# Router logits of a conv, attention and mixture-of-experts kernel: the tokens as stationary operand

## The chip, the cores and the metric

One core of one Trainium2 chip runs the whole program. The metric is the device time of one launch in microseconds (us). The core has five engines with instruction streams of their own: TensorE (PE; its weight loads are listed as PEld), VectorE (DVE), ScalarE (ACT), GpSimd (POOL) and SyncE (SP), which here only issues DMAs.

## The reference

The input `x` is 4 images of 128 channels by 1024 positions, all in float32. Three blocks follow each other.

```
x = x + Wp( softmax(q k^T / sqrt(128)) v )           # q, k, v from group_norm(x); 1024x1024 scores per image
t = tokens(x)                                        # 4 x 1024 tokens of 128 channels
t = t + linear_attention(layer_norm(t)) @ W_out + b_out   # 4 heads, softmax of the keys over the tokens
n = layer_norm(t)
logits = n @ router_w.T                              # 8 experts
rw, re = top_k(softmax(logits), 2); rw = rw / rw.sum()
ffn = n + sum_e combine[:, e] * (gelu(n @ w1[e] + b1[e]) @ w2[e] + b2[e])
out = t + ffn
```

The change concerns one line of it: `logits = n @ router_w.T`, for 4 x 1024 tokens and 8 experts.

## The kernel before

Most products are done in three parts: each float32 operand is split into a high and a low part of type fp32r, and `product3` (lines 1400 to 1405) adds high by high, high by low and low by high in one PSUM bank (128x512 float32).

The work is software-pipelined over the images. `batch(place, b, la, lc)` does three things interleaved: the convolutional attention of image b, the linear attention of image la = b-1, and the second norm, the routing and the residual of image lc = b-2. The first image has an `opening_batch`, the second a `batch` without routing, and images 2 and 3 run in a hardware loop, `with pe.Fori(2, B)` on PE and in the same way on the other engines. I call these two passes the second-image pass and the third-image pass (counting from zero). After them come the experts: for each image 16 steps (8 experts, two halves of the tokens), 64 in all, into which `TAIL_AT` puts the routing of image 2 (and the linear attention of image 3) by step number and `END_AT` the routing of image 3. The order of the work on every engine is written out by hand in these functions; nothing reorders it.

PSUM has eight banks. Everything that is not scores goes through named units in banks: `ring` 0 to 3 in the passes, and in the expert stage also two banks of `scores`. The table `LOOP_UNITS` says which bank each unit of a looped pass takes, in PE's order; in the expert stage `place_of` deals the banks out in turn, `TAIL_FIRST` being the first. `open_unit` lets PE wait until the previous unit of the same bank is drained, that is, read out by ACT or DVE. So a unit's bank decides whose reader PE waits for. In a pass the units `T0a` to `T7b` are the transposed probabilities of eight row blocks (ACT writes the high part, `turn_probs`, then DVE the low part, line 1026), `PV0/PV1` and `OT0/OT1` the attention output and its transpose (`OT` is drained by DVE's `residual`, line 1045), `g` the key-token product (drained by `take_g`), `u` and `w` the transposed first and second norm, `z` the transposed residual, `kT` the keys, `p` their softmax turned back, `c` the transposed expert shares.

The router's part of a pass runs so. When `w0` and `w1` are drained (the transposed norm, `wT_hi` and `wT_lo`, 128 channels by 1024 tokens), PE's `logits` makes two units `lg0` and `lg1`: the router, padded with zeros to 128x128 (`rt_hi`, `rt_lo`), is stationary and 512 tokens stream, three matmuls a unit. Eight of the 128 output rows are logits. ACT's `take_logits` copies 8x512 of each into `lgT`. After the scores of row block 5 and the two `u` units, PE's `turn_logits` turns them back with eight transposes of 8x128 into the unit `lT` (128 tokens by 8 tiles by 8 experts). DVE's `less_top` (lines 1143, 1144) then takes each token's maximum and subtracts it, which drains `lT`, and a chain of some twenty small DVE operations (`part_a`, `part_b`, `part_c`) finds the two best experts and their shares. In DVE's order `less_top` stands after the low parts of `T3` and before the row maximum of row block 5 (line 1019); `part_a` follows, then the key maximum, `part_b`, `part_c`, and the low parts of `T4` and `T5`. POOL's `add_bout` (line 583) waits until `z1` is filled.

Of the kernel before, what the change touches and what calls it, by code (L numbers as in the profile page):

```python
# [23 lines left out]
FP32 = mybir.dt.float32  # L24
# [8 lines left out]
E = 8  # L33
# [15 lines left out]
ROUTING = dict(o=["o0", "o1"], w=["w0", "w1"], lg=["lg0", "lg1"], z=["z0", "z1"], c=["c0", "c1"])  # L49
# [15 lines left out]
TAIL_UNITS = (ATTENTION["T"][6] + ["ctx"] + ATTENTION["T"][7] + ["m2", "m3", "PV1"] + ROUTING["o"]  # L65
              + ["OT1"] + ROUTING["w"] + LINEAR["u"] + ROUTING["lg"] + ["lT"] + LINEAR["kT"]
              + ROUTING["z"] + LINEAR["p"] + ROUTING["c"] + ["g"])

END_UNITS = (["ctx", "m2", "m3"] + ROUTING["o"] + ROUTING["w"] + ROUTING["lg"] + ["lT"]
# [20 lines left out]
LINEAR_CHAIN, ROUTING_CHAIN = 5, 17  # L90
# [42 lines left out]
def conv_attention_moe(nc, x, gn_scale, gn_bias, wq, bq, wk, bk, wv, bv, wp, bp,  # L133
# [27 lines left out]
    with ctx:  # L161
# [3 lines left out]
        def sem(name):  # L165
# [12 lines left out]
        wq_hi, wq_lo, wk_hi, wk_lo, rt_hi, rt_lo = (  # L178
            sb(n, [C, C], FP32R) for n in ("wq_hi", "wq_lo", "wk_hi", "wk_lo",
                                           "rt_hi", "rt_lo"))  # L180
# [47 lines left out]
        rr = sb("rr", [P, 6, TILES])  # L228
        comb = sb("comb", [P, 2, P])
# [8 lines left out]
        lgT = p1[0:E, :]  # L238
# [409 lines left out]
        def _(act):  # L648
# [66 lines left out]
            def take_logits(place):  # L715
                for n in range(HALVES):
                    unit = f"lg{n}"
                    wait_filled(act, place, unit)
                    act.activation(half(lgT, n), ps(place, unit)[0:E, :], ACT.Copy
                                   ).then_inc(drained[place.bank(unit)], 1)  # L720

# [41 lines left out]
            def batch(place, after_place, b, la, lc):  # L763
# [20 lines left out]
                if lc is not None:  # L784
                    take_logits(place)
# [46 lines left out]
            def experts(m, between):  # L832
# [14 lines left out]
                (TAIL_AT["lg"], lambda: take_logits(TAIL)),  # L847
# [5 lines left out]
                (END_AT["lg"], lambda: take_logits(END)),  # L853
# [9 lines left out]
        def _(dve):  # L863
# [99 lines left out]
            dve.memset(rt_hi[:, :].bitcast(FP32), 0.0)  # L963
            dve.memset(rt_lo[:, :].bitcast(FP32), 0.0)
# [17 lines left out]
            def setup_rest():  # L982
# [5 lines left out]
                after(dve.tensor_copy(rt_hi[:, 0:E], ps(FIRST, "rowsT")[:, 0:E]))  # L988
                dve.tensor_tensor(rt_lo[:, 0:E], ps(FIRST, "rowsT")[:, 0:E], rt_hi[:, 0:E].bitcast(FP32),
# [142 lines left out]
            def route(place, lc):  # L1132
# [255 lines left out]
        def _(pe):  # L1388
# [176 lines left out]
            def logits(place, lb):  # L1565
                for n in range(HALVES):
                    wait_drained(pe, place, f"w{n}")
                    whole(place, f"lg{n}", (rt_hi[:, :], rt_lo[:, :]), w_of(lb, n))

            def turn_logits(place):  # L1570
                wait_drained(pe, place, "lg0")
                wait_drained(pe, place, "lg1")
                dst = open_unit(place, "lT")
                apart(pe)
                for j in range(TILES):
                    last = pe.transpose(dst[:, j * E:(j + 1) * E], tile(lgT, j), ident[0:E, 0:E])
                fill(place, "lT", last)
# [56 lines left out]
            def batch(place, b, la, lc):  # L1634
# [41 lines left out]
                if lc is not None:  # L1676
                    turn_logits(place)
                    turn_z(place, lc)
# [17 lines left out]
            with pe.Fori(2, B) as b:  # L1696
                batch(loop_place(b), b, b - 1, b - 2)
# [100 lines left out]
```

## Time and profile before

| | |
|---|---|
| median of 3 runs | 334.31 us (334.0 to 335.09) |
| profiled execution, its own time | 334.79 us |
| its span | 332.9 us |
| busy: PE, DVE, ACT, POOL | 91%, 77%, 58%, 31% |
| chain that ended last: PE, DVE, issue, ACT | 59%, 23%, 7%, 4% |

The page of the profile divides the span among the engines, then follows the chain of work that ended last back to the start. A timeline row has the start and the length in us, the engine, the line, the operation, and in brackets how long the engine was idle before it and what ended that. PE's span can be read in five stretches: the first two images to 91.8 us, the second-image pass to 147.6, the third-image pass to 202.5, the expert stage with the TAIL work to about 265 and with the END work to about 293.5, and the rest of the experts.

### The profile page before, as it was taken

Reading aid. Unit: us, or ns where it says so; the run is one execution under the profiler, and the core shown is the slowest. Engines: PE = TensorE matmul, PEld = TensorE weight load, DVE = VectorE, ACT = ScalarE, POOL = GpSimd, SP = SyncE. Lnnn points to the kernel's source line nnn. Section 1 sums busy time; section 2 is a strip of 40 time slices with the busy share of each in tenths; the row PEclk is TensorE's granted clock in tenths of the full one; section 3 lists DMA queues with packets and bytes.
Section 4 is the critical chain, followed back from the end, with each engine's and each line's share of the span. In section 5 each row is a group of like instructions: output and inputs, shape, how many; then the busy total and the mean of one; then the engine's idle time right before and its main releaser. Section 6 shows DMA issues by size and latency. Waiting matters only on the chain.

```text
span 332.9 us, 5172 instructions
## 1 busy us (share of the span) xinstructions
PE 301.8 (91%) x1569; PEld 235.6 (71%) x1569; DVE 256.0 (77%) x623; ACT 191.8 (58%) x332; POOL 102.1 (31%) x154
## 2 busy tenths in 40 slices
PE   2887989989989899789989996999999997999995
PEld 2776868777968677577768785867757774666884
DVE  4799686678686798987687885787688685777995
ACT  3356474676570586445277656458567435856883
POOL 2345350059102664500636200089120037000000
PEclk9999999999999999999999999999999999999999
DMA  5902000010000011000000106396520692239511
GB/s 152 300 0 66 0 1 2 0 66 0 0 3 0 0 65 64 2 12 0 0 1 0 63 12 201 132 376 255 172 91 0 177 372 112 71 116 385 189 33 63
DMA packets 12757, 29.58 MB, mean 89 GB/s; under 512 B 2192, under 2 KB 5952, under 8 KB 10816
## 3 DMA queue, kind: packets, MB, share of 16 engines
q1 hardware_dynamic: 12448, 29.00, 25.3%
q10 hardware_dynamic: 288, 0.33, 0.3%
q8 instruction: 10, 0.16, 0.2%
q14 instruction: 11, 0.09, 0.1%
HBM read 24.73 MB, written 4.59 MB: 88 GB/s over the span
## 4 chain that ended last, share of the span: by engine, by line
PE 59%; DVE 23%; issue 7%; ACT 4%; DMA 3%; POOL 2%; SPq 1%; DVEq 0%; POOLq 0%; ACTq 0%
PE ring L1403 7%; PE ring L1721 6%; PE ring L1405 6%; PE ring L1404 6%; PE ring L1418 6%; PE scores L1403 6%; PE scores L1405 6%; PE scores L1404 6%; DVE prob L1019 4%; DVE pT_lo L1026 4%; PE ring L1555 2%; DVE lst L1056 2%; ACT prob L674 2%; PE ring L1533 2%; DVE t L1045 1%
## 5 line engine op out<-in xcount | busy, mean ns | idle before, releaser
L819 ACT ACTIVATE gel<-scores,b_c 128x512 f32<-128x512 f32 x64 | 43.9, 688 | 35.6 <-PE scores L1405 32.5
L1019 DVE TENSOR_SCALAR_CACHE_REDUCE prob<-scores 128x1024 f32<-128x1024 f32 x32 | 38.9, 1215 | 12.1 <-PE scores L1405 12.0
L1026 DVE TENSOR_TENSOR pT_lo<-ring,pT_hi 128x512 fp32r<-128x512 f32 x64 | 40.7, 681 | 8.1 <-ACT pT_hi L680 7.6
L556 POOL TENSOR_SCALAR rstd<-lmv 128x8 f32<-128x8 f32 x8 | 2.1, 260 | 135.3 <-DVE lmv L1062 135.3
L680 ACT ACTIVATE pT_hi<-ring 128x512 fp32r<-128x512 f32 x64 | 34.3, 598 | 14.5 <-PE ring L1418 14.5
L674 ACT ACTIVATE prob<-prob,row_max 128x1024 f32<-128x1024 f32 x32 | 36.8, 1151 | 9.5 <-DVE prob L1019 9.3
L1418 PE MATMUL ring<-ident,prob 128*128 128x128 f32 x256 | 33.9, 276 | 8.2 <-ACT prob L674 5.8
L1418 PEld LDWEIGHTS ring<-ident,prob 128*128 128x128 f32 x256 | 28.4, 140 | 14.0 <-ACT prob L674 6.1
L1403 PE MATMUL scores<-wT_hi,w_hi 128*128 128x512 f32 x64 | 34.2, 534 | 0.0
L1403 PE MATMUL scores<-k_both,q_hi 128*128 128x512 f32 x64 | 27.3, 427 | 0.9 <-DVE k_both L1004 0.9
L1403 PE MATMUL ring<-pT_hi,v_hi 128*128 128x512 f32 x64 | 26.7, 417 | 1.2 <-DVE pT_lo L1026 1.2
L1404 PE MATMUL scores<-wT_lo,w_hi 128*128 128x512 f32 x64 | 25.1, 393 | 0.0
L1405 PE MATMUL scores<-k_both,q_lo 128*128 128x512 f32 x64 | 25.1, 393 | 0.0
L1405 PE MATMUL scores<-wT_hi,w_lo 128*128 128x512 f32 x64 | 25.1, 392 | 0.0
L1404 PE MATMUL scores<-k_both,q_hi 128*128 128x512 f32 x64 | 25.1, 392 | 0.0
L1405 PE MATMUL ring<-pT_hi,v_lo 128*128 128x512 f32 x64 | 25.0, 390 | 0.0
L1404 PE MATMUL ring<-pT_lo,v_hi 128*128 128x512 f32 x64 | 25.0, 390 | 0.0
L684 ACT ACTIVATE o_s<-ring 128x512 f32<-128x512 f32 x8 | 4.8, 598 | 30.4 <-PE ring L1405 30.4
L564 POOL TENSOR_SCALAR u<-t,rstd 128x128 f32<-128x128 f32 x32 | 16.4, 531 | 0.9 <-POOL rstd L560 0.9
L1403 PEld LDWEIGHTS scores<-wT_hi,w_hi 128*128 128x128 f32 x64 | 12.1, 189 | 6.1 <-issue 4.3
L1404 PEld LDWEIGHTS scores<-wT_lo,w_hi 128*128 128x128 f32 x64 | 12.1, 189 | 5.4 <-issue 4.3
L1403 PEld LDWEIGHTS ring<-pT_hi,v_hi 128*128 128x128 f32 x64 | 12.0, 188 | 4.9 <-issue 1.2
(297 smaller groups left out, 725.9 us busy)
## 6 DMA issues: line engine op xcount, KB each, us to landing
pT_hi<-scratch_s SPq DMA_DIRECT2D x8, 1024.0 KB, 6.6
prob<-scratch_s SPq DMA_DIRECT2D x4, 1024.0 KB, 7.7
k_both<-scratch_s SPq DMA_DIRECT2D x3, 1024.0 KB, 6.7
z_in<-scratch_z SPq DMA_DIRECT2D x8, 256.0 KB, 3.2
out_dram<-out_s SPq DMA_DIRECT2D x8, 256.0 KB, 2.2
xb<-in_x_dram SPq DMA_DIRECT2D x3, 512.0 KB, 3.1
scratch_z<-out_s SPq DMA_DIRECT2D x2, 512.0 KB, 2.8
k_both<-scratch_s SPq DMA_DIRECT2D x4, 256.0 KB, 4.4
```

What stands on the lines that cost most here:

```text
L564: last = pool.tensor_scalar(dst[:, j, :], src[:, j, :], neg[:, j:j + 1], std[:, j:j + 1], ALU.add, ALU.mult)
L674: act.activation(prob[:, i % 2, :], prob[:, i % 2, :], ACT.Exp, bias=row_max[:, i:i + 1], scale=-1.0, accum_out=row_sum[:, 0, i:i + 1]).th ...
L680: act.activation(tile_group(pT_hi, n, i), as_tiles(ps(place, unit)), ACT.Copy).then_inc(p_hi_made, 1)
L819: act.activation(half(gel, s % 2), scores[:, s % 2, :], ACT.Gelu, bias=b1_c[:, s % E:s % E + 1]).then_inc(e_gelu, 1)
L1019: dve.tensor_scalar(prob[:, i % 2, :], scores[:, 2 * (i % 2):2 * (i % 2) + 2, :].rearrange("p a t -> p (a t)"), -1.0, None, ALU.mult, ALU. ...
L1026: dve.tensor_tensor(tile_group(pT_lo, n, i), as_tiles(ps(place, unit)), tile_group(pT_hi, n, i).bitcast(FP32), ALU.subtract).then_inc(drai ...
L1056: last = dve.bn_stats(lst[:, j, :], src[:, j, :])
L1403: pe.matmul(dst, lh, rh, start=start, stop=False)
L1404: pe.matmul(dst, lh, rl, start=False, stop=False)
L1405: return pe.matmul(dst, ll, rh, start=False, stop=stop)
L1418: last = pe.transpose(dst[0:t.shape[-1], j * step:j * step + rows], t, ident[0:rows, 0:rows])
L1721: last = pe.matmul(dst, tile(w2_s, e), hs_ring[step % RING], start=False, stop=e == E - 1)
```

## The change

`logits` is turned round. For each of the eight tiles of 128 tokens, the tokens are stationary and the router streams as 16 columns: first `wT_hi` against `[high, low]`, then `wT_lo` against `[high, 0]`, both into the same 16 columns of `lT`. The tokens come out on the partitions, so `lg0`, `lg1`, `take_logits` and `turn_logits` are gone. The high-part and low-part columns are added by a new DVE reduction into `logit` (64 values a partition), and `less_top` now reads that from SBUF. `lT` is filled at the place of `logits` and its bank is used again by `u1`. The table `LOOP_UNITS` is dealt anew behind `T2b`, `TAIL_FIRST` is 0 in place of 2, and PE's hardware loop over images 2 and 3 is written out.

```diff
-                  lg0=0, lg1=1, T3a=2, T3b=3, u0=0, u1=1, lT=2, z0=3, z1=0, kT0=1, kT1=2, PV0=3, T4a=0,
-                  T4b=1, T5a=2, T5b=3, p0=0, p1=1, c0=2, c1=3, g=0, OT0=1)
-TAIL_FIRST = 2
+                  lT=0, T3a=1, T3b=2, u0=3, u1=0, z0=1, z1=2, kT0=3, kT1=0, PV0=1, T4a=2, T4b=3, T5a=0,
+                  T5b=1, p0=2, p1=3, c0=0, c1=1, g=2, OT0=3)
+TAIL_FIRST = 0
...
-LINEAR_CHAIN, ROUTING_CHAIN = 5, 17
+LINEAR_CHAIN, ROUTING_CHAIN = 5, 18
...
+        router4 = sb("router4", [C, 4, E], FP32R)
+        logit = sb("logit", [P, TILES, E])
...
-            dve.memset(rt_hi[:, :].bitcast(FP32), 0.0)
-            dve.memset(rt_lo[:, :].bitcast(FP32), 0.0)
+            dve.memset(router4[:, 3, :].bitcast(FP32), 0.0)
...
-                after(dve.tensor_copy(rt_hi[:, 0:E], ps(FIRST, "rowsT")[:, 0:E]))
-                dve.tensor_tensor(rt_lo[:, 0:E], ps(FIRST, "rowsT")[:, 0:E], rt_hi[:, 0:E].bitcast(FP32),
+                router_hi, router_lo = router4[:, 0, :], router4[:, 1, :]
+                dve.tensor_copy(router4[:, 2, :], ps(FIRST, "rowsT")[:, 0:E])
+                after(dve.tensor_copy(router_hi, ps(FIRST, "rowsT")[:, 0:E]))
+                dve.tensor_tensor(router_lo, ps(FIRST, "rowsT")[:, 0:E], router_hi.bitcast(FP32),
...
-                    logits = ps(place, "lT")[:, 0:TILES * E].rearrange("p (j e) -> p j e", e=E)
-                    link("routing", lc, red(top, logits, AX.X, ALU.max, negate=True))
-                    tt(less, logits, over(top), ALU.add).then_inc(drained[place.bank("lT")], 1)
+                    parts = ps(place, "lT")[:, 0:2 * TILES * E].rearrange("p (j k e) -> p j e k", k=2, e=E)
+                    link("routing", lc, red(logit[:, :, :], parts, AX.X, ALU.add))
+                    link("routing", lc, red(top, logit[:, :, :], AX.X, ALU.max, negate=True))
+                    tt(less, logit[:, :, :], over(top), ALU.add).then_inc(drained[place.bank("lT")], 1)
...
             def logits(place, lb):
+                dst = open_unit(place, "lT")
+                both, high = (router4[:, 2 * n:2 * n + 2, :].rearrange("p k e -> p (k e)") for n in range(2))
                 for n in range(HALVES):
                     wait_drained(pe, place, f"w{n}")
-                    whole(place, f"lg{n}", (rt_hi[:, :], rt_lo[:, :]), w_of(lb, n))
-
-            def turn_logits(place):
-                wait_drained(pe, place, "lg0")
-                wait_drained(pe, place, "lg1")
-                dst = open_unit(place, "lT")
-                apart(pe)
-                for j in range(TILES):
-                    last = pe.transpose(dst[:, j * E:(j + 1) * E], tile(lgT, j), ident[0:E, 0:E])
+                    for j in range(QUAD):
+                        i = n * QUAD + j
+                        cols = dst[:, i * 2 * E:(i + 1) * 2 * E]
+                        pe.matmul(cols, wT_hi[:, bass.ds(lb * T + i * P, P)], both, start=True, stop=False)
+                        last = pe.matmul(cols, wT_lo[:, bass.ds(lb * T + i * P, P)], high, start=False, stop=True)
                 fill(place, "lT", last)
...
-            with pe.Fori(2, B) as b:
+            for b in range(2, B):
                 batch(loop_place(b), b, b - 1, b - 2)
```

## Rows read from the trace of the kernel before

**Rows 1.** The chain that ended last: shares of the span by engine
```profile
PE 59%; DVE 23%; issue 7%; ACT 4%; DMA 3%; POOL 2%; SPq 1%; DVEq 0%; POOLq 0%; ACTq 0%
```
**Rows 2.** Waits of PE between 90 and 202 us: total in us, times, longest
```profile
PE ring L1418 <- ACT p L705: 1.3, 1, 1.3
```
**Rows 3.** Timeline of the second-image pass around the logits
```profile
122.52 0.40 PE L1403 MATMUL ring<-wT_hi,rt_hi 128*128 x1
...
123.90 1.04 PE L1418 MATMUL ring<-ident,prob 128*128 128x128 f32 x8
...
125.20 1.29 DVE L1026 TENSOR_TENSOR pT_lo<-ring,pT_hi 128x512 fp32r<-128x512 f32 x2
...
127.12 0.66 PE L1576 MATMUL ring<-ident,p 8*128 8x8 f32 x8
127.71 0.86 PEld L1418 LDWEIGHTS ring<-ident,t 128*128 128x128 f32 x8
...
127.81 0.22 DVE L1143 TENSOR_REDUCE rr<-ring 128x8 f32<-128x64 f32 x1 [1.33 <-PE ring L1576]
128.07 0.22 DVE L1144 TENSOR_TENSOR rt<-ring,rr 128x64 f32<-128x64 f32 x1
128.28 1.23 DVE L1019 TENSOR_SCALAR_CACHE_REDUCE prob<-scores 128x1024 f32<-128x1024 f32 x1
...
128.89 2.38 POOL L583 TENSOR_TENSOR t<-t,bout_row 128x1024 f32<-128x1024 f32 x1 [4.37 <-PE ring L1418]
...
129.52 1.80 DVE L1149 TENSOR_SCALAR rt<-rt 128x64 f32<-128x64 f32 x1
```
**Rows 4.** Weight loads around a product with one column
```profile
17.96 0.30 PEld L1412 LDWEIGHTS ring<-cols,ctx_s 128*128 128x128 f32 x2
18.18 0.19 PEld L1403 LDWEIGHTS scores<-k_both,q_hi 128*128 128x128 f32 x1
```
**Rows 5.** Second-image pass, DVE's routing and what follows it
```profile
136.82 1.13 POOL L548 TENSOR_SCALAR xb<-xb,cols 128x1024 f32<-128x1024 f32 x1
...
137.01 1.00 DVE L1157 TENSOR_TENSOR rt<-rt,rr 128x64 f32<-128x64 f32 x1
...
141.31 2.48 DVE L1026 TENSOR_TENSOR pT_lo<-ring,pT_hi 128x512 fp32r<-128x512 f32 x4
```
**Rows 6.** Timeline from the second-image pass into the third-image pass
```profile
147.60 1.04 PE L1418 MATMUL ring<-ident,prob 128*128 128x128 f32 x8
148.14 1.13 DVE L1045 SCALAR_TENSOR_TENSOR t<-ring,row_sum,xT 128x128 f32<-128x128 f32 x4 [0.48 <-PE ring L1418]
148.24 1.08 ACT L680 ACTIVATE pT_hi<-ring 128x512 fp32r<-128x512 f32 x2 [2.03 <-PE ring L1418]
...
149.21 1.15 ACT L674 ACTIVATE prob<-prob,row_max 128x1024 f32<-128x1024 f32 x1
149.32 0.51 PE L1403 MATMUL ring<-h_hi,wq_hi 128*128 128x512 f32 x1 [0.46 <-DVE t L1045]
...
150.58 1.09 PE L1418 MATMUL ring<-ident,prob 128*128 128x128 f32 x8 [0.29 <-ACT prob L674]
```
**Rows 7.** Third-image pass: low parts of T4 and T5
```profile
193.34 2.48 DVE L1026 TENSOR_TENSOR pT_lo<-ring,pT_hi 128x512 fp32r<-128x512 f32 x4
```
**Rows 8.** The chain between the third-image pass and the experts
```profile
202.78 3.97 DMA k_both<-scratch_s
```
**Rows 9.** The last steps of the routing of image 3, PE and DVE
```profile
282.70 0.51 PE L1403 MATMUL ring<-wT_hi,rt_hi 128*128 128x512 f32 x1 [0.59 <-DVE wT_lo L995]
...
287.63 0.22 DVE L1143 TENSOR_REDUCE rr<-scores 128x8 f32<-128x64 f32 x1
...
293.45 0.33 PE L1418 MATMUL ring<-ident,comb 128*128 128x128 f32 x1 [0.42 <-DVE comb L1179]
```
**Rows 10.** A DVE operation with two SBUF operands beside POOL's, TAIL
```profile
242.12 2.19 DVE L1152 TENSOR_TENSOR rt<-rt,rr 128x64 f32<-128x64 f32 x1
```
**Rows 11.** DVE's split of the router in the first image's batch
```profile
27.61 0.16 DVE L988 CAST rt_hi<-ring 128x8 fp32r<-128x8 f32 x1
```

More of the change, by code:

```diff
@@ L48 @@
 LINEAR = dict(u=["u0", "u1"], kT=["kT0", "kT1"], p=["p0", "p1"])
-ROUTING = dict(o=["o0", "o1"], w=["w0", "w1"], lg=["lg0", "lg1"], z=["z0", "z1"], c=["c0", "c1"])
+ROUTING = dict(o=["o0", "o1"], w=["w0", "w1"], z=["z0", "z1"], c=["c0", "c1"])
 FIRST_UNITS = dict(q0=3, k0=0, k1=1, q1=2, wvT=3, wpv=0, bias_o=1, v0=2, v1=3, T0a=0, T0b=1, l1qT=2,
@@ L59 @@
                   OT1=1, v0=0, v1=1, T0a=2, T0b=3, T1a=0, T1b=1, xT0=2, xT1=3, w0=0, w1=1, T2a=2, T2b=3,
[L60 to L64 removed]
+                  lT=0, T3a=1, T3b=2, u0=3, u1=0, z0=1, z1=2, kT0=3, kT1=0, PV0=1, T4a=2, T4b=3, T5a=0,
+                  T5b=1, p0=2, p1=3, c0=0, c1=1, g=2, OT0=3)
+TAIL_FIRST = 0
 TAIL_UNITS = (ATTENTION["T"][6] + ["ctx"] + ATTENTION["T"][7] + ["m2", "m3", "PV1"] + ROUTING["o"]
[L66 removed]
+              + ["OT1"] + ROUTING["w"] + LINEAR["u"] + ["lT"] + LINEAR["kT"]
               + ROUTING["z"] + LINEAR["p"] + ROUTING["c"] + ["g"])
[L69 removed]
+END_UNITS = (["ctx", "m2", "m3"] + ROUTING["o"] + ROUTING["w"] + ["lT"]
              + ROUTING["z"] + ROUTING["c"])
@@ L177, in conv_attention_moe @@
         wpv = sb("wpv", [C, C])
-        wq_hi, wq_lo, wk_hi, wk_lo, rt_hi, rt_lo = (
-            sb(n, [C, C], FP32R) for n in ("wq_hi", "wq_lo", "wk_hi", "wk_lo",
-                                           "rt_hi", "rt_lo"))
+        wq_hi, wq_lo, wk_hi, wk_lo = (sb(n, [C, C], FP32R) for n in ("wq_hi", "wq_lo", "wk_hi", "wk_lo"))
+        router4 = sb("router4", [C, 4, E], FP32R)
         bout_row = sb("bout_row", [P, C])
@@ L713, in turn_keys @@
                                    ).then_inc(drained[place.bank(unit)], 1)
[L715 to L720, printed above, removed]
             def route_exp(place, lb):
@@ L783, in batch @@
                 turn_probs(place, 2)
-                if lc is not None:
-                    take_logits(place)
                 turn_probs(place, 3)
@@ L846, in _ @@
                 *((TAIL_AT["u" + str(n)], lambda n=n: turn_u(TAIL, n)) for n in range(2)),
-                (TAIL_AT["lg"], lambda: take_logits(TAIL)),
                 (TAIL_AT["exp"], lambda: route_exp(TAIL, lc)),
@@ L852, in _ @@
                 *((END_AT["w" + str(n)], lambda n=n: turn_normed(END, "w", n, w_halves(la), w_hi_made)) for n in range(2)),
-                (END_AT["lg"], lambda: take_logits(END)),
                 (END_AT["exp"], lambda: route_exp(END, la)),
@@ L1676, in batch @@
                 if lc is not None:
-                    turn_logits(place)
                     turn_z(place, lc)
@@ L1753, in _ @@
                 (TAIL_AT["lg"], lambda: logits(TAIL, lc)),
-                (TAIL_AT["lT"], lambda: turn_logits(TAIL)),
                 (TAIL_AT["kT"], lambda: keys(TAIL)),
@@ L1765, in _ @@
                 (END_AT["lg"], lambda: logits(END, la)),
-                (END_AT["lT"], lambda: turn_logits(END)),
                 (END_AT["z"], lambda: turn_z(END, la)),
```

1 line of the change is left out of this document (removed).

## The prediction

> **What bounds the kernel now.** I read the page's engine shares first, then the chain that ended last, then PE's waits, then the timeline around each place that the diff touches. PE is busy nine tenths of the span and carries 59% of the chain, DVE 23% [rows 1]. In the expert stage the chain is nearly all PE. In the two looped passes it changes sides: PE streams, but at the logits the chain leaves PE and stays on DVE for 15 us. The reader sees it in the timeline: PE's eight small transposes end at 127.71, DVE, which had idled 1.33 us for them, takes the maximum at once, subtracts, and only then does the row maximum of block 5 [rows 3]. DVE then works through routing, key maximum and shares until the low parts of T4 and T5 [rows 5], on which the share transposes and the next scores wait. PE meanwhile has slack of its own: one wait of 1.3 us for the key softmax [rows 2]. From the third-image pass into the experts the chain runs over DVE's share copy, stores and a broadcast load of 3.97 us [rows 8], not over PE.
>
> **PE's own work.** Removed for each image: six matmuls of 512 columns, 122.52 to 123.90, 1.38 us, and eight transposes, 127.12 to 127.71, 0.59 us [rows 3]. Added: sixteen pairs of a 128x128 load and a 16-column matmul. The nearest row is a product with one column: its two loads span 0.30 at 0.19 each, so they start 0.11 apart, and the next load follows after another 0.11 [rows 4]. A pair thus costs a load, 0.112, however short the matmul: 16 x 0.112 = 1.79 us. Lower bound: the pace of the small transposes, 0.59 / 8 = 0.074, gives 1.18. Upper bound: loads not overlapped at all, 0.19 each [rows 4], gives 3.04. I take 1.79, its row having the same 128x128 operand. So PE's gain is 0.18 us an image, with 0.41 more at the logits and 0.59 less later.
>
> The Trainium skill, "TensorE: Matmul & The Clock Gate", section "Back-to-back issue gap", lists matmuls of 1 to 64 columns at about 60 cycles, 25 ns; by that the sixteen would be an estimated 0.4 us. Its section on LDWEIGHTS gives columns / 1.2 in ns, 107 for 128, and says that the row count doesn't matter; [rows 4] agree with 107, the eight-row transposes of [rows 3] came faster than it allows. The first would make the change a gain; it is the first rival below, which has its price from rows.
>
> **DVE's own work.** One reduction more. Line 1143 reads 64 values a partition in 0.22 and the next starts 0.26 later [rows 3]; the new one reads 128. Line 1026 does 512 in about 0.62 (1.29 for two, [rows 3]), 1.2 ns each, so 64 more are 0.07: 0.33 a step (between 0.26 and 0.52). `less_top` becomes 0.33 + 0.26 + 0.22 = 0.81 us. Its last operation now has both operands in SBUF. Such an operation took 2.19 us beside a POOL operation [rows 10] instead of 0.22; here POOL has been idle 4.37 us before line 583 [rows 3], so I cost the wait at nothing; if POOL moved there it would be up to 2.2. The skill's page "SBUF — State Buffer", section "Who interferes with whom", states the same as a rule: a DVE instruction with two SBUF inputs contends with a GpSimd instruction that reads SBUF.
>
> **The two looped passes.** The sixteen pairs make T3's transposes 0.41 late, and ACT's high and DVE's low parts with them: the low parts end at about 126.90 instead of 126.49 (125.20 + 1.29). `less_top` needs nothing more from PE, so `lT` is drained at 126.95 + 0.81 = 127.75. Two things follow. DVE's row maximum starts at about 127.8 instead of 128.28, 0.5 early. But `u1` now sits in `lT`'s bank: PE would be ready for it at 127.0 and waits until 127.8; with its four transposes of 0.109 `z` starts at 128.24 instead of 127.71, 0.5 late. POOL's `add_bout` starts on `z1`, hence also 0.5 late, 129.4, and ends at 131.75.
> DVE then gets the first operation of `part_a` in before POOL (it had stood 1.80 us behind POOL, [rows 3]) but a later one with two SBUF operands stands until POOL's end, itself 0.5 later. In the second-image pass every further POOL operation is 0.5 late too, and each holds one DVE operation, as line 1157 was held till the end of line 548, 137.95 [rows 5]. Going through them one by one, four more short operations fit in under cover before POOL's end at 138.4; the low parts of T4 start at 141.1 instead of 141.31: -0.2. In the third-image pass DVE is bound by ACT's high part of T4, which hangs on PE's 0.5: 193.25 instead of 193.34 [rows 7]: -0.1. Bounds for each: -0.5 (DVE keeps all of it) and +0.5 (PE's lateness decides). PE's 0.5 at the end of the third pass lies behind the stores and the load of [rows 8].
>
> **The bank table between the two passes.** The new table ends a pass with `g` in bank 2 and `OT0` in bank 3, and begins the next with `T6a` in 2 and `T6b` in 3. Before, `OT0`'s bank went to `q0`, and one sees PE stand there 0.46 us until line 1045 is done, at 149.27 [rows 6]. Now `T6b` stands there. Its four transposes start at 149.33 instead of 148.04 (147.60 and four times 0.11); ACT's second copy of T6 starts at 149.95, the exponential of block 7 at 150.47 instead of 149.21, and T7's transposes, which wait for it at 150.58 [rows 6], at 151.83. `q0`, whose bank is free now, moves up but its ACT copy stands behind the exponential, so `k0` is late as well. That is +1.25 us, with 15 us of unbroken PE work behind it. Bounds: 0 and 1.4. It happens once: the pass before the loop ends on the old banks, and `TAIL_FIRST` 0 gives T6 the banks of `c0` and `c1`, long drained.
>
> **Experts.** TAIL: PE loses 0.59 and gains 0.41, on the chain: -0.2. END: the second half of the logits starts when `w1` is drained, 282.70 [rows 9]; eight pairs are about 0.15 longer than three matmuls, and with them the GELU and DVE's start on the routing at 287.63. From there DVE works unbroken to the shares, PE waiting 0.42 for them [rows 9]; the new reduction adds 0.33. The 0.59 of the removed transposes only lengthens that wait. END: +0.45.
> **The rest.** One more 128x8 copy on DVE's busy stretch in the first image, 0.16 long and partly overlapped [rows 11]: +0.1. ACT's two copies an image lie in ACT's idle time: nothing; were ACT late there, 1.2 us back. The written-out PE loop: at its edge T6's transposes at 147.60 have no idle time before them [rows 6], so nothing to gain; bounds -0.3 and +0.3.
>
> **Sum.** 0.1 - 0.2 + 1.25 - 0.1 - 0.2 + 0.45 = +1.3 us. The profiled execution took 334.79 (span 332.9), so 336.1 in its terms; the median of before is 334.31, so I predict 335.6.
>
> **Rivals.**
> Short loads: the pair runs at the small transposes' 0.074. Then TAIL gains 0.6 more, END 0.3, the passes 0.2 each: 335.6 - 1.3 = 334.3. For it: load and 16 columns are short. Against: [rows 4]. Chance 0.14.
> The bank wait is covered: T7's delay is taken up before DVE's next work: 335.6 - 1.25 = 334.35. Against: PE runs unbroken after 150.58. Chance 0.15.
> The other side, faster: POOL's block. In both passes line 1149 stood about 1.6 us behind `add_bout` (1.80 for an operation of 0.2). If DVE, 0.5 earlier, gets all five operations of `part_a` (1.3 us) in before POOL's start, each pass gains 1.6 instead of 0.15: 335.6 - 2.9 = 332.7. It decides if POOL starts after 130.3; I have 129.4. Chance 0.12.
> Slow loads: 0.19 a pair. TAIL +1.25, END +0.6, the passes about 0.8 each: 339.1. Chance 0.09.
> My forecast has 0.50, its own range 334.9 to 336.6.
>
> **How the numbers follow.** A change under 0.3%, 1 us, can't be told from none here; the limits are 333.3 and 335.3. Slower: 0.43 of my case, slow loads and a little of the rest, 0.53. Same: the two 334.3 cases and the lower edge of mine, 0.33. Faster: POOL's case and edges, 0.14. The range leaves out slow loads and most of POOL's case: 333.4 to 337.6.
>
> **What would show it.** In the trace after: sixteen matmuls of 16 columns 0.11 apart; PE idle before `u1`, ended by `rt` (line 1144's successor), 0.7 to 0.8 us, in both passes; PE idle about 0.7 us or more before `T6b` ended by DVE `t`, once, and T7 of that pass waiting for ACT over 1.2 us later than now; DVE's row maximum of block 5 no longer behind `z`; in END PE's wait for `comb` 1.2 us instead of 0.42. I am wrong if the pairs are not load-bound, if the second-to-third pass distance does not grow, or if DVE's `part_a` runs free of POOL.

## The result and the profile after

| | before | after |
|---|---|---|
| median of 4 runs each | 334.15 us (333.57 to 335.09) | 338.27 us (337.24 to 338.94) |
| profiled execution, span | 334.79, 332.9 us | 338.56, 336.5 us |
| granted clock of PE, mean of the span | 1.0 | 0.99 |

The changed kernel is slower: the ratio is 1.0115 with a 95% interval of 1.0091 to 1.0139, some 3.8 us (the medians lie 4.1 apart). I had forecast 335.6 and a range up to 337.6. The sign is right, the size is not.

The page of after: busy shares, the chain (its shares stand against [rows 1]), and the granted clock in tenths over 40 slices.

```profile
PE 303.2 (90%) x1577; PEld 238.1 (71%) x1577; DVE 257.2 (76%) x627; ACT 187.7 (56%) x324; POOL 101.9 (30%) x154
PE 64%; DVE 21%; issue 6%; ACT 5%; POOL 2%; DMA 1%; DVEq 0%; ACTq 0%; POOLq 0%
PEclk9999999999999999989999999999999999899999
```

The last of these lines holds what I had not looked for: two of the 40 slices are an 8 instead of a 9. The text comes back to them below. First the steps that I had foreseen. The pairs of load and matmul of the second-image pass, PE's timeline (to be read against [rows 3] and [rows 4]):

```profile
122.34 0.26 PE L1565 MATMUL ring<-router,wT_lo 128*128 128x16 f32 x1
122.45 0.26 PE L1564 MATMUL ring<-router,wT_hi 128*128 128x16 f32 x1
122.56 0.26 PE L1565 MATMUL ring<-router,wT_lo 128*128 128x16 f32 x1
...
123.90 0.26 PE L1565 MATMUL ring<-router,wT_lo 128*128 128x16 f32 x1
```

Load and matmul together go at one every 0.11 us. The first of the sixteen starts at 122.31 and the work behind them at 124.01: 1.70 us. In the same pass, the engines around `u1` (PE first, then DVE, then POOL):

```profile
127.48 0.63 PE L1408 MATMUL ring<-ident,u 128*128 128x128 f32 x4 [0.55 <-DVE rt L1134]
...
126.54 0.28 DVE L1132 TENSOR_REDUCE logit<-ring 128x64 f32<-128x128 f32 x1
...
128.92 0.16 DVE L1139 TENSOR_SCALAR rt<-rt 128x64 f32<-128x64 f32 x1
129.12 2.41 DVE L1140 TENSOR_TENSOR rt<-rt,falling 128x64 f32<-128x64 f32 x1
...
129.07 2.38 POOL L582 TENSOR_TENSOR t<-t,bout_row 128x1024 f32<-128x1024 f32 x1 [4.84 <-PE ring L1408]
```

`u1` waits 0.55 us for `less_top`. DVE gets one operation of `part_a` in ahead of POOL (128.92), and the next stands until POOL's end (129.12 to 131.53). All this is as foreseen. Three lines of PE's timeline at the pass boundary, against [rows 6]:

```profile
148.76 0.63 PE L1408 MATMUL ring<-ident,prob 128*128 128x128 f32 x4
...
150.22 0.66 PE L1408 MATMUL ring<-ident,prob 128*128 128x128 f32 x4 [0.83 <-DVE t L1034]
...
152.69 0.55 PE L1408 MATMUL ring<-ident,prob 128*128 128x128 f32 x3 [0.89 <-ACT prob L673]
```

`T6b` now stands behind `OT0`'s reader, and T7 waits for the exponential. From the start of `OT0`'s transposes to the start of `q1` it is 155.79 - 148.12 = 7.67 us in after and 153.69 - 147.17 = 6.52 us in before: +1.15.

Then the two 8s, which are two falls of the granted clock. The stretch with the key softmax's transposes in the second-image pass, as windows (start and end, length, busy time and count of PE, PEld, DVE, ACT, POOL, then the granted clock), with the wait ahead of it:

```profile
142.00:144.00 2.00, 1.92 (x11) 1.56 (x11) 2.00 (x4) 0.79 (x2) 0.00 (x0) 0.64 0.00 0
144.00:146.00 2.00, 2.00 (x6) 1.61 (x6) 1.26 (x4) 1.50 (x3) 0.00 (x0) 0.50 0.03 8
146.00:148.00 2.00, 2.00 (x17) 1.92 (x17) 1.23 (x2) 0.15 (x2) 0.00 (x0) 1.00 0.19 49
```
```profile
142.08 1.68 PE L1408 MATMUL ring<-ident,p 128*128 128x128 f32 x8 [2.18 <-DVE pT_lo L1015]
...
144.49 0.63 PE L1394 MATMUL scores<-k_both,q_hi 128*128 128x512 f32 x1
144.91 0.63 PE L1395 MATMUL scores<-k_both,q_lo 128*128 128x512 f32 x1
```

The same windows of before have the clock at 1.00. In after PE is granted 0.50 of full speed, that is the lower of its two levels (1.2 instead of 2.4 GHz): matmuls of 512 columns start 0.42 apart where 0.23 is usual. And in the experts:

```profile
284.00:286.00 2.00, 1.79 (x12) 1.65 (x13) 1.36 (x3) 0.22 (x1) 0.00 (x0) 0.98 0.00 0
286.00:288.00 2.00, 2.00 (x5) 0.89 (x3) 1.16 (x2) 1.21 (x2) 0.00 (x0) 0.50 0.00 0
288.00:290.00 2.00, 2.00 (x7) 1.41 (x5) 0.74 (x2) 0.47 (x1) 0.00 (x0) 0.66 0.15 56
```
```profile
278.89 0.66 PE L1408 MATMUL scores<-ident,w_n 128*128 128x128 f32 x4 [1.85 <-POOL w_n L563]
...
284.21 0.28 PE L1564 MATMUL ring<-router,wT_hi 128*128 128x16 f32 x1 [0.49 <-DVE wT_lo L984]
```

The two profiles can be compared stretch by stretch, as distances between the starts of the same PE work (after less before):

| stretch | after less before, us |
|---|---|
| first images, up to `q0` of the second-image pass (93.31 and 93.64) | -0.3 |
| second-image pass, up to `OT0` | +1.3, of which the fall +1.0 |
| boundary, `OT0` to `q1` | +1.15 |
| third-image pass, up to its `OT0` | +0.3 |
| TAIL, up to END's m3 product | -0.9 |
| END, up to `comb`'s transposes | +2.05, of which the fall 1.65 |

They add up to the 3.6 us between the spans. The first row is no effect that can be told: profiles of kernels with the code of before differ by up to 1.1 us there. What a fall costs is read from later profiles with the same waits and full clock: 53.8 us for the pass where after has 54.8, and 27.9 for END where after has 29.5. Without the two falls the rest behind `q0` is +1.2, near my +1.3. The falls are the other 2.7.

### The profile page after: what moved, and what is told of

The parts are those of the page before. It is cut to its first block, busy times and chain, and to the rows that moved or that the text cites. A ratio compares the mean times of both kernels' runs of the same rounds, so it can differ in the third digit from the quotient of the medians.

```text
span 336.5 us, 5099 instructions
## 1 busy us (share of the span) xinstructions
PE 303.2 (90%) x1577; PEld 238.1 (71%) x1577; DVE 257.2 (76%) x627; ACT 187.7 (56%) x324; POOL 101.9 (30%) x154
## 4 chain that ended last, share of the span: by engine, by line
PE 64%; DVE 21%; issue 6%; ACT 5%; POOL 2%; DMA 1%; DVEq 0%; ACTq 0%; POOLq 0%
PE ring L1408 7%; PE ring L1393 7%; PE ring L1709 7%; PE ring L1395 6%; PE ring L1394 6%; PE scores L1393 6%; PE scores L1395 6%; PE scores L1394 6%; DVE prob L1008 3%; DVE pT_lo L1015 3%; PE ring L1545 2%; PE ring L1523 2%; DVE lst L1045 2%; ACT prob L673 2%; PE ring L1510 2%
## 5 line engine op out<-in xcount | busy, mean ns | idle before, releaser
L1393 PE MATMUL scores<-wT_hi,w_hi 128*128 128x512 f32 x64 | 35.6, 556 | 0.7 <-ACT gel L809 0.7
L1393 PE MATMUL scores<-k_both,q_hi 128*128 128x512 f32 x64 | 27.8, 435 | 0.9 <-DVE k_both L993 0.9
L1394 PE MATMUL scores<-k_both,q_hi 128*128 128x512 f32 x64 | 25.3, 396 | 0.0
```

What stands on the lines that cost most here:

```text
L1393: pe.matmul(dst, lh, rh, start=start, stop=False)
L1394: pe.matmul(dst, lh, rl, start=False, stop=False)
```

## The experiments

An execution has a mean granted clock of 0.998 or more, of 0.993 to 0.995, or of 0.990. The profiled ones of these groups show no fall, one fall and two falls. So I count executions at 0.996 or less as "with a fall"; where it lies, only the profiled ones tell. The kernel before, run again beside every experiment, has 13 of 104; their median is 335.4 us against 334.0 for the rest, so a fall costs about 1.4 us in it. I call the kernel of the next run, the change with a bank table that keeps its new waits out, the one with the sound table.

**The bank table undone.** The changed logits stay; the units behind `T2b` get banks that leave `T6b` clear of `OT0` and `u1` clear of `lT`.

```diff
-                  lT=0, T3a=1, T3b=2, u0=3, u1=0, z0=1, z1=2, kT0=3, kT1=0, PV0=1, T4a=2, T4b=3, T5a=0,
-                  T5b=1, p0=2, p1=3, c0=0, c1=1, g=2, OT0=3)
-TAIL_FIRST = 0
+                  lT=0, T3a=2, T3b=3, u0=1, u1=2, z0=3, z1=0, kT0=1, kT1=2, PV0=3, T4a=0, T4b=1, T5a=2,
+                  T5b=3, p0=0, p1=1, c0=2, c1=3, g=0, OT0=1)
+TAIL_FIRST = 2
```

> The changed kernel with a bank table that keeps lT out of u1's way (T3a=2, T3b=3, u0=1, u1=2) and ends a pass as before (g=0, OT0=1), TAIL_FIRST 2. Theory (bank waits plus two falls of the granted clock): PE's wait of 0.55 us before u1 and of 0.83 us before T6b are gone, the distance from the second to the third pass shrinks by 1.1 us; PE is then even earlier at the key transposes, waits there for DVE over 2 us, and the granted clock still falls, in the pass and at the end of the routing of image 3: about 337.1 us. Rival 1 (the bank table is all of it): 334.5. Rival 2 (the written-out loop or the DVE reduction is what costs): 338.2, unchanged.

Measured: 334.56 us, ratio 1.0004 (0.9984 to 1.0023), 4 of 12 executions with a fall. The first rival was right, and my theory that both falls would stay was wrong: the table was the price. All the rest of the change costs between -0.5 and +0.8 us, nothing that can be told. The profile has full clock in the pass, and it shows what the table had changed there. PE's eight transposes of `u` run through, POOL starts at 128.32, and DVE's operation stands behind it as it did before:

```profile
126.32 1.04 PE L1408 MATMUL ring<-ident,u 128*128 128x128 f32 x8
...
128.90 1.84 DVE L1139 TENSOR_SCALAR rt<-rt 128x64 f32<-128x64 f32 x1
...
128.32 2.37 POOL L582 TENSOR_TENSOR t<-t,bout_row 128x1024 f32<-128x1024 f32 x1 [4.10 <-PE ring L1408]
```

In this kernel PE waits twice later on (1.3 for ACT's `p`, then 1.2 for DVE's `pT_lo`), as in before [rows 2]. In after, whose pass starts 0.33 sooner in its profile than in that of before (93.31 and 93.64), DVE got ahead and delivered the key maximum sooner: ACT's `p` starts at 135.85 (before 136.88, so 0.7 sooner in the pass). PE's wait for it vanishes, and PE stands one long wait of 2.18 ahead of `p0` instead, since the low parts it waits for begin at 141.25 (before 141.31, so 0.27 later in the pass). This chain from `u1`'s bank to the long wait is read from the profiles; a table with `u1` alone behind `lT` was not tried. `T6b`'s wait can't be its cause, as it comes 8 us later. The last windows of END still show a fall here (282 to 286), behind a wait of 0.5:

```profile
280.00:282.00 2.00, 1.51 (x14) 1.42 (x13) 2.00 (x4) 0.65 (x2) 0.24 (x1) 1.00 0.00 0
282.00:284.00 2.00, 2.00 (x10) 1.66 (x10) 0.58 (x1) 0.21 (x1) 0.00 (x0) 0.66 0.00 0
284.00:286.00 2.00, 2.00 (x4) 0.97 (x3) 1.49 (x3) 0.99 (x2) 0.00 (x0) 0.50 0.00 0
```

**The loop written out, in the kernel before.**

```diff
-            with pe.Fori(2, B) as b:
+            for b in range(2, B):
```

> The kernel before with PE's loop over images 2 and 3 written out and nothing else. Theory: no effect, 334.2 within 0.5 us, clock 1.0 throughout. Rival (the longer instruction stream is fetched late and PE stands for it): 335.5 to 337, with PE idle times that no semaphore ends in the two passes.

Measured: 334.94, ratio 1.0019 (0.9999 to 1.0039), 4 of 12 with a fall. That is between nothing and 0.4%, a little over what I had expected, and the clock was not full throughout as I had said. The run before holds the written-out loop too and leaves it at most 0.8 us of the 3.8. The opposite half, the changed logits inside the hardware loop, was not tried.

**Only the bank wait, in the kernel before.**

```diff
-                  ... p0=0, p1=1, c0=2, c1=3, g=0, OT0=1)
-TAIL_FIRST = 2
+                  ... p0=0, p1=1, c0=0, c1=1, g=2, OT0=3)
+TAIL_FIRST = 0
```

> The kernel before, its router untouched, with only the last banks of a pass dealt as in the changed kernel (c0=0, c1=1, g=2, OT0=3, TAIL_FIRST 0), so that T6b of the next pass waits for OT0's reader. Theory: PE stands 0.8 us before T6b once, T7 follows 1.1 to 1.3 us late, and nothing takes it back: 335.3 to 335.5. Rival (covered by later slack): 334.2.

Measured: 335.47, ratio 1.0036 (1.0019 to 1.0053), +1.1 us, 2 of 12 with a fall. PE's waits in the two passes now have the new one:

```profile
PE ring L1418 <- DVE t L1045: 0.9, 1, 0.9
```

So the predicted term is real by itself: +1.1 us (0.6 to 1.8) against +1.25, as expected before the run. Falls are no more frequent than in the kernel before.

**PE kept busy ahead of the long wait of the pass.** The changed kernel with the last three-part product of score block 6 done twice more in the second- and third-image passes (it writes the same values).

```diff
+                for _ in range(2 if i == 6 and not (isinstance(b, int) and b < 2) else 0):
+                    last = product3(scores[:, 2 * (i % 2) + 1, :], (tile(q_hi, i), tile(q_lo, i)),
+                                    (half(k_hi, 1), half(k_lo, 1)))
```

> The changed kernel; in the two looped passes PE computes the last three-part product of the scores of row block 6 twice more into the same bank (6 matmuls, 1.4 us), where it stands 2.2 us for DVE's low parts of T4. Theory (the long wait lets the granted clock fall to half, and the next 3.4 us of matmuls run at 0.43 instead of 0.23 us each): clock 1.0 through the second-image pass, the pass about 1 us shorter although it has more work, total 337.2; the fall in the routing of image 3 stays. Rival (the clock falls for another reason, and PE's idle time is just slack): the fall stays, total 338.3 or more.

Measured: 337.21, ratio 1.0086 (1.006 to 1.0113), 1 of 6 with a fall. The wait of 2.2 is down to 0.8, the clock in the pass is 1.00 throughout, and from the pass's first product to `OT0`'s transposes it is 53.8 us, where before has 53.5 and after 54.8. But the added work costs about 1.4 us in the third pass, where nothing had waited so long. It shows the fall of the pass hanging on the wait (1 of 6 executions with a fall, against 10 of 10 of the changed kernel, counted below), and that filling the wait with useless work isn't a cure. One part of my expectation failed: the fall in END should have stayed, and it was gone too, though END was not touched and PE's waits there are the same:

```profile
PE scores L1408 <- POOL w_n L563: 1.8, 1, 1.8
PE ring L1567 <- DVE wT_lo L984: 0.5, 1, 0.5
```
```profile
286.00:288.00 2.00, 2.00 (x9) 1.30 (x8) 0.96 (x2) 1.21 (x2) 0.00 (x0) 1.00 0.00 0
```

So these waits alone don't make END's fall. Why it came in most executions of the changed kernel and in at most one of these six, the runs don't show.

**The router streamed wide.** 64 columns in place of 16, 48 of them zero, at the same 0.11 a pair.

```diff
-        router4 = sb("router4", [C, 4, E], FP32R)
+        router4 = sb("router4", [C, 16, E], FP32R)
...
-                        cols = dst[:, i * 2 * E:(i + 1) * 2 * E]
+                        cols = dst[:, i * 8 * E:(i + 1) * 8 * E]
```

> The changed kernel with the router streamed as 64 columns (48 of them zero) in place of 16, same loads, same pace of 0.11 us a pair since the load covers 64 columns. Theory A (the sixteen pairs leave the array nearly idle, and that with the 0.5 us wait between the halves is what lets the clock fall in the routing of image 3): fewer falls there, 1 to 1.5 us less than the changed kernel. Theory B (the falls come from true idle time of PE before them): nothing changes, 338. If the pairs become longer than 0.11 us, they were not bound by the loads.

Measured: 338.04, ratio 1.0104 (1.0077 to 1.013), 4 of 6 with a fall. Its profiled execution falls in the pass, with the same wait of 2.2:

```profile
142.00:144.00 2.00, 1.85 (x11) 1.23 (x11) 2.00 (x4) 1.20 (x2) 0.00 (x0) 0.82 0.00 0
144.00:146.00 2.00, 2.00 (x6) 1.61 (x6) 1.26 (x4) 1.09 (x2) 0.00 (x0) 0.50 0.03 8
```

The width of the stream doesn't decide in the pass. In END this profile has waits of 2.0 and 0.5 and full clock. With the sound table and 64 columns:

> The changed kernel with the bank table mended and the router streamed as 64 columns (48 of them zero) in place of 16, so that each pair of load and matmul has four times the columns at the same pace of loads. If the fall of the granted clock in END (4 of 12 executions with 16 columns) comes from the short streams, it is gone: 333.4 to 334.3, all executions at 0.998 or more. If it comes from the waits ahead of and behind the logits, a third of the executions keep it and the median stays at 334.3 to 335.0. If the wide matmuls no longer hide behind the loads (pairs over 0.112 apart), it costs 0.5 us or more in five places: 335 or more.

Measured: 333.81, ratio 0.9998 (0.9978 to 1.0018), 3 of 12 with a fall, against 4 of 12 with 16 columns. Nor does it in END, as far as twelve executions can tell.

**PE kept busy ahead of END's w turn.** The changed kernel, the hidden product of step 34 done three times.

```diff
-                product3(scores[:, s % 2, :], (tile(w1_hi, e), tile(w1_lo, e)), w_of(m, h)).then_inc(e_h, 1)
+                for _ in range(3 if m * 2 * E + s == 34 else 1):
+                    last = product3(scores[:, s % 2, :], (tile(w1_hi, e), tile(w1_lo, e)), w_of(m, h))
+                last.then_inc(e_h, 1)
```

> The changed kernel with the expert product of step 34 computed three times into the same bank (6 matmuls more, 1.4 us), where PE stands 1.85 us for POOL's second norm of image 3. Theory B (idle time of PE lets the clock fall): the fall in the routing of image 3 is gone or rare, 1.2 to 1.7 us less than the changed kernel. Theory A (the narrow products do it by themselves): it stays, and the time is that of the changed kernel.

Measured: 336.74, ratio 1.0089 (1.0057 to 1.012), 4 of 6 with a fall; the profiled one has none, though its pass has the wait of 2.2 too:

```profile
PE ring L1408 <- DVE pT_lo L1015: 3.0, 3, 2.2
```
```profile
144.00:146.00 2.00, 2.00 (x14) 1.76 (x13) 1.72 (x5) 1.24 (x2) 0.00 (x0) 1.00 0.03 8
```

Such a wait makes the fall likely, not certain. One of the six has a mean of 0.99, as with two falls, though END's long waits are gone; no profile says where its second one lay. Its two executions without a fall took 334.95 and 335.03, under my 335.6; a part of that is the repeat's own gain, as the next runs show.

**The two together.** Sound table and the repeated product.

> The changed kernel with the bank table mended (T6b no longer behind OT0) and the hidden product of step 34 in END done three times (the repeats write the same values; about 0.6 us of added PE work in all). My theory: the mended table left one loss, a fall of PE's granted clock to half in END in 4 of 12 executions, worth about 1.1 us each; with PE kept busy ahead of END's logits no execution shows it, mean clock 0.998 or more in all, median 333.4 to 334.3, ratio to before 0.998 to 1.000. Rival, the fall comes from the sixteen narrow products themselves: it stays in a third of the executions and the added work is paid on top, 335.0 or more. Rival, the fall only moves to another place: mean clock 0.995 in some executions with no fall at END's logits in the profile, 334.5 to 335.5.

Measured: 333.46, ratio 0.9976 (0.9966 to 0.9986), no fall in 11 executions. It beats even the kernel before, by 0.24%. Was that the changed logits? The same repeat in the kernel before, and this kernel once more beside it:

> The kernel before with the hidden product of step 34 in END done three times, as in the run with the mended table. It tells whether the 0.24% of that run belongs to the added products or to the changed logits with a sound table. My theory: in the kernel before most executions hold full clock through END already, so the repeats have nothing to save; they lie in a wait of PE for w or cost up to 0.6 us: 334.2 to 334.8, ratio 0.999 to 1.002. Rival, the repeats alone make the gain (they shift END's order): 333.5, ratio 0.9976, and the changed logits with a sound table are worth nothing.

> The changed kernel with the mended table and the repeated product of step 34 once more, beside the one above on the same chip. My theory: ratio 0.997 to 0.999 again, all executions at 0.998 or more. If the first result was chance, 0.999 to 1.001.

Measured: 332.96, ratio 0.9954 (0.9932 to 0.9976), 0 of 7 with a fall; and 333.38, ratio 0.9967 (0.9952 to 0.9981), 0 of 11. The rival was right: the repeat makes the gain, and the kernel before gains as much. My reading of the repeat as a cure for the clock alone falls as well. DVE and POOL of the kernel before in END, first without the repeat:

```profile
279.13 2.37 POOL L574 TENSOR_TENSOR t<-t,w_n 128x1024 f32<-128x1024 f32 x1
...
279.49 2.55 DVE L1303 TENSOR_TENSOR hw<-gel,k_both 128x512 f32<-128x512 f32 x1
281.97 0.68 DVE L995 TENSOR_TENSOR wT_lo<-scores,wT_hi 128x512 fp32r<-128x512 f32 x1
```

and with it:

```profile
278.12 2.84 POOL L574 TENSOR_TENSOR t<-t,w_n 128x1024 f32<-128x1024 f32 x1
...
278.02 0.69 DVE L1303 TENSOR_TENSOR hw<-gel,k_both 128x512 f32<-128x512 f32 x1
279.41 0.69 DVE L995 TENSOR_TENSOR wT_lo<-scores,wT_hi 128x512 fp32r<-128x512 f32 x1 [0.70 <-ACT wT_hi L699]
```

The operation to watch is `hw`. Its start stands 0.36 behind POOL's in the one and 0.10 ahead of it in the other, and it takes 2.55 or 0.69 us. What lets it get ahead lies 4 us earlier. Here is the step before, in the kernel before (DVE's previous `hw`, one of POOL's eight `w_n` operations, PE's transposes of the first four):

```profile
275.40 0.73 DVE L1303 TENSOR_TENSOR hw<-gel,k_both 128x512 f32<-128x512 f32 x1 [0.86 <-ACT gel L819]
...
275.59 0.88 POOL L564 TENSOR_SCALAR w_n<-t,rstd 128x128 f32<-128x128 f32 x1
...
277.38 0.66 PE L1418 MATMUL scores<-ident,w_n 128*128 128x128 f32 x4 [1.87 <-POOL w_n L564]
```

and with the repeat:

```profile
275.73 0.69 DVE L1303 TENSOR_TENSOR hw<-gel,k_both 128x512 f32<-128x512 f32 x1 [2.22 <-ACT gel L819]
...
275.83 0.91 POOL L564 TENSOR_SCALAR w_n<-t,rstd 128x128 f32<-128x128 f32 x1
...
275.91 0.66 PE L1418 MATMUL scores<-ident,w_n 128*128 128x128 f32 x4
```

An operation of `w_n` takes 0.45 us, but 0.88 or 0.91 where DVE's `hw` has started just before it. In the kernel before, this is the second operation, so the fourth ends 0.43 late, and with it PE's wait. The six more matmuls fit in the 1.87 that PE waited, and they make the GELU and `hw` later: now `hw` holds up the fifth operation, which the transposes don't need. They start 1.79 behind the start of `w_n` (274.12 to 275.91) instead of 2.23 (275.15 to 277.38), both times 0.05 behind the end of the fourth operation (275.86 and 277.33). With that 0.44 DVE slips in ahead of POOL at the next `hw`. `wT_lo` is there in time, PE's wait of 0.59 [rows 9] is gone, and from END's m3 product to `comb`'s transposes it is 26.5 us instead of 27.5.

**The same wait filled with useful work.** If the order was all, one more real step there should do as well. END's w turns at steps 35 and 35, or 35 and 36, in place of 34 and 35, in the kernel before and in the changed one with the sound table.

```diff
-END_AT = dict(ctx=25, m2=27, m3=28, o=29, st=29, w0=34, w1=35, lg=36, ...
+END_AT = dict(ctx=25, m2=27, m3=28, o=29, st=29, w0=35, w1=35, lg=36, ...
```

> The kernel before with the first w turn of END at step 35 instead of 34 (both turns at step 35), nothing repeated. PE then has one more hidden product and its w2 product (about 1.5 us) to do in the 1.87 us wait for POOL's w_n. My theory: what the repeated product gave came from the order of DVE and POOL: the wait shrinks to 0.4 or less, hw takes 0.69 instead of 2.55, the wait of 0.59 for wT_lo goes; from m3's product to the shares' transposes 26.5 instead of 27.5 and the useful work is not paid twice: 332.0 to 333.3. Rival, full clock needed the added work: the waits go but the time stays within 0.3% of 334.3. Rival, both turns at one step make DVE late: its wT_lo of the second half falls behind POOL again, 334 or more.

> The changed kernel with the mended table and the same move of the first w turn to step 35. My theory: as for the kernel before, 0.4 us above it: 332.4 to 333.7, no execution under clock 0.998. If the clock needs the added work: falls in a third of the executions and 334.3 or more.

> The kernel before with END's w turns at steps 35 and 36 (from 34 and 35). The second turn, a step later, shares its step with the logits, whose second half then waits for DVE's low part right behind its turn: my theory 0.5 to 1.0 us of that wait comes back, 332.8 to 334.0, a little slower than with both turns at 35. Rival: the step between the turns keeps DVE ahead of POOL and it is the faster of the two, by 0.5 or more.

> The changed kernel with the mended table and END's w turns at steps 35 and 36. My theory: as the kernel before with the same steps, within 0.5 us, 333.0 to 334.3; with a wait of 0.5 or more ahead of the second eight narrow matmuls the clock falls in some executions (0.995 or less), which would show that it is the wait beside the narrow matmuls and not the missing repeat that decides.

Measured: 334.82 (1.0004 to 1.0034), 8 of 12 with a fall; 335.18 (1.0005 to 1.0042), 9 of 12; 336.81 (1.0059 to 1.0099), 5 of 6; 336.88 (1.0075 to 1.0142), 6 of 6. My expectation failed in all four, and they are the best evidence on the clock. (For the last of them I had named the other outcome too: falls behind a wait of 0.5 or more.) In the first, `hw` is free of the long POOL operation (0.89) and the 0.59 is gone, as I had said. But the second turn, now right behind the first, waits for POOL. PE's wait for `w_n` from 264 us on, and the windows:

```profile
PE scores L1418 <- POOL w_n L564: 2.0, 2, 1.5
```
```profile
278.00:280.00 2.00, 1.59 (x6) 1.50 (x7) 0.27 (x1) 0.52 (x1) 1.92 (x2) 0.63 0.00 0
280.00:282.00 2.00, 2.00 (x5) 1.00 (x3) 1.22 (x2) 1.28 (x3) 0.80 (x1) 0.51 0.00 0
```

There isn't one narrow matmul near: four transposes stand between waits of 0.47 and 1.49, and the clock is halved behind them. Four executions kept the clock and took 333.73 in the median, eight fell and took 334.95: 1.2 us for the fall. But 333.73 is also the time of the kernel before beside them (333.75), so the useful work at this place gained nothing even at full clock: to get `hw` clear of POOL isn't enough by itself, and what the new wait of 1.49 takes back wasn't measured alone. In the third kernel DVE's second `wT_lo` does fall behind POOL and PE waits 2.7 us; the windows behind it show 0.50:

```profile
282.00:284.00 2.00, 0.37 (x1) 0.37 (x2) 1.57 (x2) 0.00 (x0) 0.42 (x1) 0.85 0.00 0
284.00:286.00 2.00, 2.00 (x6) 1.52 (x6) 0.00 (x0) 0.59 (x1) 0.00 (x0) 0.50 0.00 0
```

**END's routing a step earlier.** The sound table with `lT=37, rA=37, exp=37` in place of 38.

> e1_table with the routing of image 3 one step earlier on DVE and ACT (lT, rA, exp at step 37 instead of 38), which the missing transposes allow. Theory: DVE takes the nine operations in its idle time before the multiply of step 38, PE's wait for the shares (0.4 to 0.5 us) goes, 0.8 to 1.2 us less than e1_table: 333.5, faster than before by 0.7. Rival (DVE becomes late with its multiplies, or the two table loads on ACT now delay the GELUs): 334.6 or more.

Measured: 335.5, ratio 1.0047 (1.0029 to 1.0066), 2 of 6 with a fall; its four others took 335.77 in the median, so this cost has another source than the clock, which I haven't looked for. I had expected 333.5; the rival (334.6 or more) held.

**The changed kernel again**, beside new executions of the kernel before:

> The changed kernel once more, for more executions of it on the chip of the experiments: how many show a granted clock below 1.0 and how long these are against the others. Theory (bank wait and DVE's reduction about +1.3, the rest is the clock): executions at 1.0 lie at 335.5 to 337, those with one fall 1.2 to 1.5 above, those with two as much again; before shows a fall in about a quarter of its executions, this in most. Rival (the clock is not the difference): its executions at clock 1.0 lie at 338 too.

Measured: 338.39, ratio 1.0132 (1.0113 to 1.0152), 6 of 6 with a fall, five of them with two. In its profile both lie at the same places as in the first.

Put in one table, with PE's waits in us as the profiles have them (the longest ones ahead of the places of the two falls):

| kernel | key softmax of the second-image pass | END's w turns and logits | with a fall |
|---|---|---|---|
| before | 1.3 and 1.1 | 1.9 and 0.6 | 13 of 104 |
| before, bank wait | 1.3 and 1.1 | as before | 2 of 12 |
| before, loop written out | as before | 1.8 and 0.6 | 4 of 12 |
| before, repeat in END | as before | none | 0 of 7 |
| sound table (16 or 64 columns) | 1.3 and 1.2 | 1.8 or 1.9, and 0.5 | 7 of 24 |
| sound table, repeat in END | 1.3 and 1.2 | none | 0 of 22 |
| sound table, routing a step earlier | 1.3 and 1.2 | 1.8 and 0.5 | 2 of 6 |
| after | 2.2 | 1.8 and 0.5 | 10 of 10, seven with two |
| after, wide | 2.2 | 2.0 and 0.5 | 4 of 6, two with two |
| after, repeat in END | 2.2 | 0.2 | 4 of 6, one with two |
| after, blocks repeated in the pass | 0.8 | 1.8 and 0.5 | 1 of 6 |
| w turns at 35, 35 (both kernels) | as their own | 0.5 and 1.5 | 17 of 24 |
| w turns at 35, 36 (both kernels) | as their own | 0.5, then 2.7 or 2.6 | 11 of 12 |

The length of a wait isn't the whole condition. At the start of the experts every profile has PE waiting 1.64 us for ACT's `prob` and, in the kernel before, 0.75 and 0.61 soon after (202 to 208 us), and none of the eighteen shows a fall there. What else decides is open.

## Why the prediction was wrong in size

**PE's own work** held: 0.11 a pair, sixteen in 1.70 where I had 1.79. The two rivals on the load (0.074, 0.19) are out. The Trainium skill, "TensorE: Matmul & The Clock Gate", section "Back-to-back issue gap", gives the 25 ns, from which I had estimated 0.4 us, for a matmul by itself; the same section says that in a stream of pairs the spacing is set by the load and the matmul together. The trace agrees with that: 0.11 a pair with 16 columns and with 64. **DVE's own work** held: `less_top` runs from 126.54 to 127.33, 0.79 against 0.81, and L1140, with two inputs in SBUF, took 2.41 beside POOL where before has 0.24 for it. The Trainium skill, "SBUF — State Buffer", section "Who interferes with whom", states that a DVE instruction with two SBUF inputs contends with a GpSimd instruction that reads SBUF, and the trace agrees.

**The two passes**: `u1` waits 0.55, where I had 0.7 to 0.8, and for the reason that I had given. POOL's `add_bout` is 0.5 late in the pass, as I had it (129.07, and the 0.33 of the earlier start), and the rival of POOL's block didn't come: one operation got in, not five. Apart from the clock the second pass is +0.24 where I had -0.2, and the third, to the start of its `OT0`, is +0.3 where I had -0.1. The low parts of `T4`, on which I had hung both, began 0.27 later from `q0` in the one and 0.12 later from `q1` in the other, not 0.2 and 0.1 sooner.

**The bank table** held: +1.15 in the profile and +1.1 alone, against +1.25. It wasn't covered. **TAIL** gave -0.9 (-0.6 in the second profile of the changed kernel), more than -0.2. Half of it is a wait of PE for DVE's `m` that the kernel before has and the changed one, at 209.74, has not:

```profile
207.79 2.05 PE L1555 MATMUL ring<-m,uT 128*128 128x128 f32 x16 [0.61 <-DVE m L1092]
```

**END** gave +0.4 without its fall, against +0.45; PE's wait for `comb` isn't 1.2, as I had written, but 0.48, because PE now waits 0.72 for a GELU just before: together 1.2.

With the measured sizes my sum is +1.2 instead of +1.3 (0.24 + 1.15 + 0.3 - 0.9 + 0.4). That they agree so well is luck: three terms are off by 0.4 to 0.7 us and nearly cancel, and the +0.1 for the first image can't be told from the -0.3 of that stretch. No execution of after kept the full clock to test the sum; the nearest are the wide router's two at 335.46 and 336.95, and the run with blocks repeated in the pass, 337.2 less the 1.4 that these cost, 335.8. They fit a forecast of 335.6 for full clock and don't prove it.

The step that failed is one that every term shares: I priced each wait of PE at its length, and took the granted clock as full, without a word on it. "**The two looped passes**" went through DVE's queue operation by operation and found its own gain, and never asked what PE's two waits of before (1.3 and 1.12) turn into when ACT's `p` comes 0.7 us sooner and `pT_lo` doesn't. They turn into one of 2.18. As a wait that costs no time, but behind it the clock is halved for 3 us in most executions (+1.0 in the profile). The second fall, in END, wasn't to be read from the profile of before, which has the waits of 1.87 and 0.59 and full clock throughout; seven executions of eight of before go so. It is worth +1.65 in the profile, and seven of ten executions of after have two falls. Why it comes more often in after than in the kernel with the sound table (7 of 24) or in the one with the pass filled (1 of 6), whose END has the same waits, I can't say; the runs don't settle it. Nor do they settle what sixteen short matmuls add beside the waits: 16 and 64 columns did not differ.

## What to carry over

When banks are dealt anew, list for every unit whose reader it now waits for; here the entries that put `T6b` behind `OT0` cost 1.1 us alone, and the whole table, with `u1` behind `lT` and the falls, 3.7, while the matmuls that the change was about were worth nothing that can be told. Be wary of an edit that merges two waits of the busiest engine into one, even where the sum stays, and count the executions by their mean clock, not only the median, before and after. And an edit that seems to work for one reason wants its control in the old kernel: the repeated product helped that as much. Last, a change in one wait is to be followed up the chain until an operation of another length is found: the 0.44 us of `w_n` came from one POOL operation of 0.88.

## What the runs showed of the hardware

The granted clock halves behind waits of PE that are still short beside the span: in these profiles behind one of 2.18, one of 2.7, and pairs of 0.47 and 1.49 or of 1.85 and 0.49, for about 3 us each time, at 1.2 to 1.4 us a fall between medians (1.0 and 1.65 in the profile). It differs from one execution to the next: the same wait of 2.18 passed without a fall in one profile, and so did one of 1.64 at the start of the experts in all. DVE and POOL hold each other up in both directions: a POOL operation of 0.45 us on `w_n` took 0.88 and 0.91 behind a DVE operation with two inputs in SBUF that had started 0.19 and 0.10 earlier. Two DVE operations of the same form took 0.69 and 2.55 us, according to whether they started 0.10 before or 0.36 behind POOL's start.
